# MLP of a Mamba-2 kernel on one core: one of four remainders moved from GpSimd to VectorE

## The reference, cut to what matters

```python
# x: (8, 1024, 256); first a two-layer Mamba-2 block, then:
h = x
for blk in range(3):
    i0, i1 = (2 * blk, 2 * blk + 1)
    y = _qlora_linear(h, qweights[i0], scales[i0], biases[i0], lora_a[i0], lora_b[i0])
    y = _layernorm(y, ln_gamma[blk], ln_beta[blk])
    y = jax.nn.gelu(y, approximate=False)
    y = _qlora_linear(y, qweights[i1], scales[i1], biases[i1], lora_a[i1], lora_b[i1])
    h = y + h
return h
# around it: x = x + _L0_ffn_ref(_layernorm(x, axis=-1), ...)
```

## Time and profile before

| what | value |
|---|---|
| median of 3 runs | 1781.3 us (1776.38 to 1782.0) |
| the profiled execution | 1781.56 us, span 1779.8 us |
| TensorE's mean granted clock | 0.978 of full |
| busy share: PE, PEld, DVE, ACT, POOL | 92%, 73%, 77%, 71%, 67% |
| remainders of h on POOL, L1777 | 96, mean 1362 ns, 129.3 us busy |
| remainders of g on POOL, L1784 | 96, mean 1337 ns, 126.5 us busy |

### The profile page before, as it was taken

How to read it: one execution, slowest core, us unless ns; L and a number is a source line. 1 busy time by engine, 2 the same in 40 slices (tenths; PEclk the granted TensorE clock), 3 DMA queues, 4 the chain that set the end, 5 groups by cost and what they waited for, 6 DMA issues and landing times. The chain is left out here.

```text
span 1779.8 us, 35344 instructions
## 1 busy us (share of the span) xinstructions
PE 1637.6 (92%) x12440; PEld 1290.7 (73%) x12440; DVE 1369.8 (77%) x2941; ACT 1268.5 (71%) x1999; POOL 1183.8 (67%) x1022
## 2 busy tenths in 40 slices
PE   5799999999999998999999999999987799999998
PEld 4477777777777776777776777777766688888887
DVE  6787778888887776777888888777775796868755
ACT  3677777777777774777777777777761677777785
POOL 2477776777777773665566666665532797979785
PEclk9899999999999998999999999999996899999999
DMA  4011111111111111111112111111150304031101
GB/s 162 19 48 43 43 41 41 56 62 41 41 41 47 41 42 36 48 43 43 43 53 64 41 41 41 47 41 41 29 160 32 99 1 143 1 109 35 36 13 48
DMA packets 87045, 91.67 MB, mean 52 GB/s; under 512 B 4928, under 2 KB 82224, under 8 KB 86960
## 3 DMA queue, kind: packets, MB, share of 16 engines
q1 hardware_dynamic: 80512, 79.94, 13.9%
q10 hardware_dynamic: 6448, 10.63, 2.5%
HBM read 57.00 MB, written 25.17 MB: 46 GB/s over the span
## 5 line engine op out<-in xcount | busy, mean ns | idle before, releaser
L1025 POOL TENSOR_TENSOR L_xc<-L_xpad,L_vec 128x512 f32<-128x512 f32 x160 | 166.2, 1039 | 313.2 <-ACT L_xpad L814 237.2
L498 PE MATMUL L_front<-L_uhi,L_whi 128*128 128x512 f32 x568 | 243.8, 429 | 9.2 <-DVE L_xc L1302 4.7
L666 PE MATMUL L_mix<-L_wo,L_yg 128*128 128x256 f32 x1024 | 240.7, 389 | 0.0
L853 ACT ACTIVATE L_dbank<-L_dbank 128x1024 f32<-128x1024 f32 x128 | 129.2, 1009 | 143.9 <-PE L_dbank L559 143.1
L498 PE MATMUL L_front<-L_uhi,L_wlo 128*128 128x512 f32 x568 | 226.4, 399 | 0.0
L498 PE MATMUL L_front<-L_ulo,L_whi 128*128 128x512 f32 x568 | 225.7, 397 | 0.0
L1315 DVE TENSOR_TENSOR L_m<-L_dbank,L_gm 128x1024 f32<-128x1024 f32 x128 | 156.3, 1221 | 84.2 <-ACT L_dbank L855 84.2
L666 PEld LDWEIGHTS L_mix<-L_wo,L_yg 128*128 128x128 f32 x1024 | 196.5, 195 | 28.7 <-issue 0.9
L1017 POOL TENSOR_TENSOR L_yg<-L_yg,L_sz 128x512 f32<-128x512 f32 x128 | 176.8, 1392 | 37.7 <-DVE L_yg L1331 37.7
L1036 POOL TENSOR_TENSOR L_wx<-L_dtx,L_decay 128x512 f32<-128x512 f32 x120 | 124.1, 1045 | 94.5 <-DVE L_dtx L1320 94.5
L1777 POOL TENSOR_TENSOR M_alo<-M_hT,M_ahi 128x512 fp32r<-128x512 f32 x96 | 129.3, 1362 | 46.3 <-ACT M_ahi L1710 46.3
(11 more groups left out here) (209 smaller groups left out, 4378.1 us busy)
## 6 DMA issues: line engine op xcount, KB each, us to landing
h<-L_hres SPq DMA_DIRECT2D x32, 512.0 KB, 3.0
M_first<-in_x SPq DMA_DIRECT2D x20, 512.0 KB, 4.8
M_first<-h SPq DMA_DIRECT2D x18, 512.0 KB, 4.8
L_hres<-in_x SPq DMA_DIRECT2D x16, 512.0 KB, 3.9
L_cc<-L_xc ACTq DMA_DIRECT2D x64, 128.0 KB, 2.3
L_hres<-h SPq DMA_DIRECT2D x16, 512.0 KB, 3.8
M_hin<-h SPq DMA_DIRECT2D x10, 512.0 KB, 4.4
out<-M_hin SPq DMA_DIRECT2D x10, 512.0 KB, 3.1
```

Source lines behind the costliest of these rows:

```text
L498: last = nc.tensor.matmul(to[:, :], ww[:, kd, tile * P:(tile + 1) * P], a[:, kd, :], start=i == 0, stop=i == len(passes) - 1)
L666: last = nc.tensor.matmul(mix[1 - s][:, (b % 2) * DM:(b % 2 + 1) * DM], yg[:, t, b * P:(b + 1) * P], wo[layer][:, t, :], start=t == 0, sto ...
L853: nc.scalar.activation(dbank[:, :, :], dbank[:, :, :], ACT.Abs).then_inc(d_abs, 1)
L1025: nc.gpsimd.tensor_tensor(xc[p][:, q, :].rearrange("p (b i) -> p b i", b=NB), xpad[:, q, :, 0:P], vector(layer, "conv_w", q * TAPS, 1).uns ...
```

## The change

The remainder of the second half of h is formed by VectorE, behind the first block statistics of a slot, for the next slot. GpSimd keeps the first half of h and both halves of g. The semaphore `h_lo` becomes one for each half.

```diff
-        h_hi, h_lo = sem("h_hi"), sem("h_lo")
+        h_hi, h_lo = sem("h_hi"), [sem(f"h_lo{kd}") for kd in range(KD)]
...
                     if half == 0:
-                        pe.wait_ge(h_lo, 2 * n + kd + 1)
+                        pe.wait_ge(h_lo[kd], n + 1)
...
-            def rest_h(n, kd):
+            def rest_h(n):
                 if not runs(n):
                     return
                 u = n % UNITS
-                pool.wait_ge(h_hi, 2 * n + kd + 1)
-                nc.gpsimd.tensor_tensor(alo[u][:, kd, :], hT[u][:, kd, :], ahi[u][:, kd, :].bitcast(F32), ALU.subtract).then_inc(h_lo, 1)
+                pool.wait_ge(h_hi, 2 * n + 1)
+                nc.gpsimd.tensor_tensor(alo[u][:, 0, :], hT[u][:, 0, :], ahi[u][:, 0, :].bitcast(F32), ALU.subtract).then_inc(h_lo[0], 1)
...
-                rest_h(n + 1, 0)
-                rest_h(n + 1, 1)
+                rest_h(n + 1)
...
+            def rest_h(n):
+                if not runs(n):
+                    return
+                u = n % UNITS
+                dve.wait_ge(h_hi, 2 * n + 2)
+                nc.vector.tensor_tensor(alo[u][:, 1, :], hT[u][:, 1, :], ahi[u][:, 1, :].bitcast(F32), ALU.subtract).then_inc(h_lo[1], 1)
...
                 block_stats(n, 0)
+                rest_h(n + 1)
                 in_stats(entering(n, 2, 4), 2)
                 block_stats(n, 1)
```

## The result

| | before | changed |
|---|---|---|
| median of 5 runs each | 1776.59 us (1773.32 to 1782.0) | 1825.19 us (1822.5 to 1832.58) |
| ratio, 95% interval | 1 | 1.0269 (1.0237 to 1.0301) |
| profiled execution, its span | 1781.56, 1779.8 us | 1832.58, 1830.8 us |

What follows compares the result with a forecast made beforehand. TensorE was taken to set the pace, GpSimd close behind. Three rounds +46.7, seven plain slots +2.8, the slot ahead of the rounds +1.1 and the start +3.3 made +53.9: 1835 us, 3.0% slower; range 1797 to 1855.

Steps and rivals of the forecast that it cites:

- rival C: Faster: GpSimd is what TensorE waits for, VectorE finds the rounding done, TensorE's passes alone count: 1768 us; chance 0.07.
- The ring: In the MLP, VectorE waits for ScalarE's rounding, ScalarE for GpSimd's shift, GpSimd for VectorE's variance: 7.35 us in series per pass.
- The passes of 7.35, 8.55, 9.3, 11.9 and 9.95 us: Times between shifts: plain slots; 4, 6, 8, 10 (item's statistics); 5, 7, 9 (normalised, next added); 11; entering and leaving slots.
- The price of the operation: VectorE's new remainder: 0.60 us of its queue up to 1.7, about 0.68 free, at most 1.09 waiting at the port.
- Rival B: The ring is hidden: operation not held at the port, plain pass 6.78 under TensorE's 6.95: 1781 us; chance 0.07.
- The blocked normalisations: In slots 5, 7, 9, three of four normalisations are blocked 1.0 us each by GpSimd's remainders: 4.3 us, pass 9.3.
- Rival A: The ring closes, but VectorE wins the port, so slots 5, 7, 9 take 7.35: about 1812 us; chance 0.24.
- Entering and leaving: Slots 11, 0, 1, 2 of a round: between turnings of entering items 9.95 us, where TensorE before took 9.00.
- the start: Start of the MLP: the item's statistics stand behind the new operation, +1.3 twice and +0.7 for the first item: +3.3 us.
- the plain slot ahead of the first round: The slot before the three rounds, put at 6.2 us before the change: claimed +1.1 us.
- The seven plain slots: The slots following the three rounds, each going from 6.95 to 7.35 us: claimed +2.8 us.
- The sign of a wait in nearly all 48 slots: VectorE should wait for ScalarE's rounding before its new line, over 1 us each, the greatest wait of the MLP.

Runs made afterwards that it cites:

- both relieved: Against the kernel before: VectorE forms the second half's remainder behind the moments, and the entering item's normalisation goes ahead of the additions into h; 1766.96 us, ratio 0.9937.
- the experiment with it: Kernel before, with VectorE only waiting for the next slot's second rounding at the new operation's place; GpSimd forms all four remainders: 1807.52 us, ratio 1.0146.
- with the port free: Changed kernel without GpSimd's remainder of h's first half, TensorE multiplying the second half's twice instead: 1815.06 us, ratio 1.0204 to the kernel before.

## Why the prediction was right, point by point

**The bound of before** was read rightly: TensorE 6.95 and 9.0 per slot, GpSimd close behind. What I left vague was the 4 us a round above TensorE's own. The runs show them as two rows that hold each other: both relieved, a round took 91.7. So rival C's 1768 us, reckoned as if relief of GpSimd alone would give them, was too low: the remainder left out altogether gave 1774.33.

**The ring** is shown. Its wait is the greatest of the MLP, its steps are in the timeline, and plain slots went back to 6.95 each time when a piece was taken out: the statistics behind the wait, the later rounding, the port's 0.57, or the whole. The passes of 7.35, 8.55, 9.3, 11.9 and 9.95 us measured 7.27, 8.4, 9.35, 11.96 and 9.9. In the plain pass, VectorE's request was reckoned at T+3.10 and came at T+3.03, and its next instruction started at T+4.20 in place of 4.27, which is the 0.08 of the whole. (The prediction's own terms, the port at T+3.73 and 0.60 behind it, make 4.33; its 4.27 was nearer.) What I did not see is how much the wait costs alone: I expected the experiment with it at 1780 to 1792 us, and it took 1807.52.

**The price of the operation**, 0.68 free and up to 1.09 more at the port, measured 0.67 to 1.25; the forecast 1.3 for plain slots was 1.25. **Rival B** made its price too low: with the port free, as the experiment had it, plain slots did return to 6.95, but the other slots kept most of their loss and the kernel took 1815 us, not 1781.

**The blocked normalisations** are shown as three blocks (4.39 us where 4.3 was reckoned):

```profile
1450.29 4.39 DVE L1830 TENSOR_SCALAR M_later<-M_hin,M_mv,M_rstd 128x256 f32<-128x256 f32 x4
1454.60 1.21 DVE L1803 TENSOR_TENSOR M_hin<-M_hin,M_later 128x1024 f32<-128x1024 f32 x1
```

The first three of the four take 1.47, 1.38 and 1.37 us, the last 0.40. Rival A, in which VectorE wins the port, fell: the pass was 9.35.

**Entering and leaving.** TensorE's turning out stands behind the additions into h, as said:

```profile
1507.77 1.09 PE L1673 MATMUL M_lin<-M_kept,M_hT 128*128 128x128 f32 x8 [0.73 <-DVE M_hT L1865]
```

**What was off.** The sum was 5 us too high of 54. In the terms, 1.6 of it is in the rounds, mainly 0.15 in each of the twelve slots with an item's statistics and up to 0.3 in the last slot of a round (7.06 in place of 7.35). 0.9 is in the start and the slot behind it, and there one term was misread: the plain slot ahead of the first round was put at 6.2 us before, which is what slot 39 took, so +1.1 was added; slot 3 itself took 6.99 before and 7.07 changed, +0.1. 1.5 is the open ring at the end, which I had not seen: the term was missing. The seven plain slots gave the forecast +2.8 in part by luck: a pass lost 0.32 and not 0.40, and slot 40 took 6.39 before and not 6.95. The profiled pair differs by 51.0 us, the medians by 48.6; the profiled execution of the changed kernel was the slowest of its five, and where in it the 2.4 us lie is not shown. The sign of a wait in nearly all 48 slots came in 39, and GpSimd's busy time fell by 70 us and not 62.

## What to carry to other kernels

Moving an operation to an engine with idle time adds its wait to that engine's queue. Ask what already stands behind the place, and follow it round: if it feeds, over other engines, the thing waited for in the next turn, the pass of this ring has to be under the slot time of the engine that sets the pace. And where two engines share a port, first look at which operations will run side by side; here a change of order in VectorE's queue was worth nothing alone, the move of work to a better place still cost 0.35% alone, and both together gained 0.6%.

## What was not expected of the hardware

- Normalisations on VectorE, which have one tensor input, and remainders on GpSimd alternate one by one: four normalisations take 1.38 us when free, and 2.4, 3.4, 4.4 and 5.4 (once 4.98) with one to four of them held by GpSimd.
- GpSimd's small power (128x4) is lengthened too: 1.01 us alone, 1.43 to 1.45 beside VectorE's two-input subtraction, 1.57 beside that and four normalisations.
- The stage ahead of the MLP is the same code in all of these kernels, and the MLP's first addition on VectorE began between 1366.2 and 1379.5 us in their profiled executions. Differences of under some 13 us between single executions say nothing here; the times between shifts do, most of which repeat to 0.05 us from round to round.
